# The reciprocal root of three layer normalizations: Newton steps on VectorE in the place of Sqrt on ScalarE and RECIPROCAL on VectorE

## What is computed

```python
def _ln(x, g, b):
    m = jnp.mean(x, axis=-1, keepdims=True)
    v = jnp.mean((x - m) ** 2, axis=-1, keepdims=True)
    return (x - m) * jax.lax.rsqrt(v + EPS) * g + b      # EPS = 1e-05
...
h = _ln(x, pw_g[pathway_ids], pw_b[pathway_ids])
h = _ln(h, cp_g[compartment_ids], cp_b[compartment_ids])
t = _ln(x, tm_g[time_steps], tm_b[time_steps])
s = _ln(x, ms_g[scale_type], ms_b[scale_type])
cat = jnp.concatenate([w[0] * h, w[1] * t, w[2] * m, w[3] * n, w[4] * r, w[5] * s], axis=-1)
return _ln(silu(cat @ int_W1 + int_b1) @ int_W2 + int_b2, int_g, int_be)
...
x = x + attention(cond(x));  x = x + experts(stage(x))
```

## Time and profile before

| | |
|---|---|
| median of 3 runs | 2525.4 us (2524.65 to 2525.51) |
| the profiled execution | 2525.69 us |
| its span | 2523.9 us |
| mean granted PE clock | 0.853 |
| PE busy | 2141.4 us (85%) |
| DVE busy | 1360.4 us (54%) |
| ACT busy | 978.8 us (39%) |
| POOL busy | 858.3 us (34%) |

### The profile page before, as it was taken

The page is one execution under the profiler, slowest core; times in us unless marked ns, Lnnn a source line. Parts: engine busy times, 40 slices in busy tenths (PEclk is TensorE's granted clock), DMA queues, the critical chain, the costliest instruction groups (busy, mean ns, idle before and its releaser), DMA issues. The chain is left out here.

```text
span 2523.9 us, 33767 instructions
## 1 busy us (share of the span) xinstructions
PE 2141.4 (85%) x11902; PEld 1378.9 (55%) x11902; DVE 1360.4 (54%) x3618; ACT 978.8 (39%) x2423; POOL 858.3 (34%) x586
## 2 busy tenths in 40 slices
PE   6518989889889989989988988989999589798987
PEld 5305555555555555555555555556778445454545
DVE  2355766766766766766766665442111055555545
ACT  2004445535535535535535535632222133333231
POOL 0161535534534535435435432041000232424121
PEclk9557698888788788778778778999999789898989
DMA  7100021020020020020020022042445420302000
GB/s 253 44 5 14 1 70 26 1 86 26 1 86 26 1 86 26 1 86 26 1 86 26 1 76 68 1 170 72 149 161 197 150 71 1 85 0 85 0 30 18
DMA packets 67428, 145.88 MB, mean 58 GB/s; under 512 B 16356, under 2 KB 42075, under 8 KB 62947
## 3 DMA queue, kind: packets, MB, share of 16 engines
q1 hardware_dynamic: 51434, 93.79, 11.0%
q0 software_dynamic: 15872, 50.35, 6.6%
HBM read 114.64 MB, written 29.46 MB: 57 GB/s over the span
## 5 line engine op out<-in xcount | busy, mean ns | idle before, releaser
L1211 ACT ACTIVATE att_buf<-att_buf,nmin 128x384 f32<-128x384 f32 (+3 forms) x512 | 287.6, 562 | 497.1 <-DVE nmin L1571 496.7
L1021 PE MATMUL bank<-kk,qT 32*128 32x512 f32 (+2 forms) x1024 | 330.7, 684 | 42.4 <-DVE nmin L1571 41.7
L772 POOL TENSOR_TENSOR big<-ex_at,kx 128x2048 f32<-128x2048 f32 x64 | 236.2, 3713 | 237.9 <-DVE xt_na L1324 175.3
L1048 PE MATMUL bank<-ident,att_buf 128*128 128x128 f32 x1280 | 245.3, 331 | 20.9 <-ACT att_buf L1219 19.7
L1062 PE MATMUL bank<-att_buf,vp 128*32 128x128 f32 x2560 | 226.9, 316 | 0.0
L719 POOL TENSOR_TENSOR big<-kx 128x1280 f32<-128x1280 f32 x64 | 162.8, 2572 | 177.9 <-ACT kx L1125 156.7
L1560 DVE TENSOR_TENSOR att_buf<-bank,wdiag 128x128 f32<-128x128 f32 x384 | 93.0, 284 | 232.3 <-PE bank L1026 231.1
L1219 ACT COPY att_buf<-bank 128x384 f32<-128x384 f32 (+3 forms) x512 | 209.1, 409 | 14.1 <-PE bank L1062 12.0
L1048 PEld LDWEIGHTS bank<-ident,att_buf 128*128 128x128 f32 x1280 | 182.0, 174 | 34.0 <-ACT att_buf L1211 27.9
L1021 PEld LDWEIGHTS bank<-kk,qT 32*128 32x128 f32 x1024 | 111.2, 224 | 113.0 <-DVE nmin L1571 60.8
L1062 PEld LDWEIGHTS bank<-att_buf,vp 128*32 128x32 f32 x2560 | 139.3, 124 | 60.8 <-issue 50.2
(11 more groups left out here) (349 smaller groups left out, 4144.9 us busy)
## 6 DMA issues: line engine op xcount, KB each, us to landing
big<-in_eW SPq DMA_DIRECT2D x16, 1024.0 KB, 7.9
kk<-in_eW SPq DMA_DIRECT2D x16, 1024.0 KB, 7.5
buf_d<-zero SPq DMA_DIRECT2D x8, 640.0 KB, 7.6
xt_na<-in_xT SPq DMA_DIRECT2D x8, 512.0 KB, 3.4
nA<-in_xN SPq DMA_DIRECT2D x8, 512.0 KB, 3.5
x_d<-x SPq DMA_DIRECT2D x8, 512.0 KB, 3.4
x<-x_d SPq DMA_DIRECT2D x8, 512.0 KB, 4.0
out<-qf SPq DMA_DIRECT2D x8, 512.0 KB, 2.9
```

The source lines that it names most:

```text
L772: pool.tensor_tensor(pv[:, c * P:(c + 1) * P, :].rearrange("p (h d) o -> p o h d", d=DH), spread(ex[:, t, :, 8 * c:8 * c + 8], 3, DH), spr ...
L1021: pe.matmul(bank[u % 2][:, 0:n], qT[r:r + 32, g, i * P:(i + 1) * P], kk[r:r + 32, g, T * i * P:T * i * P + n], start=True, stop=False)
L1048: mm = pe.transpose(bank[3 + u % 2][:, j * P:(j + 1) * P], pr[:, u % NPR, j * P:(j + 1) * P], ident[:])
L1211: act.activation(pr[:, u % NPR, 0:n], pr[:, u % NPR, 0:n], ACT.Exp, scale=-1.0, bias=nmin[:, u % 4:u % 4 + 1], accum_out=rsum[:, i, h:h + ...
```

## The change

ACT no longer takes the root in the three normalizations; the Sqrt activations and the semaphores `varn` and `sdn` are gone. DVE makes the reciprocal root itself, in `moments`, right behind the statistics: it adds eps to the variance, takes a first guess by arithmetic on the number's bits (-0.5 times the bits read as an integer, plus a constant), and betters it by three Newton steps, y <- y (1.5 - 0.5 w y y), of three instructions each. That makes eleven instructions on 128x4 numbers, with a wait for DVE's own last result ahead of each. The reciprocal in `normed` is gone. The slots in `AT` of all other steps are as before.

```diff
--- before.py
+++ after.py
@@ -1142,22 +1142,13 @@
                                                        bias=obcol[:, o:o + 1], scale=pc1[:, 4 + o:5 + o])
 
                                 def router_stream():
-                                    sd = lambda n: act.activation(mv[:, :, 2:3], mv[:, :, 1:2], ACT.Sqrt, bias=eps_ln[:, 0:1])\
-                                        .then_inc(s(f"sd{n}"), 1)
-
                                     def out_of_bank(n):
                                         for m in range(K2):
                                             act.wait_ge(s("cat_mm"), 2 * n + m + 1)
                                             act.copy(cat[:, 2 * n + m, :], bank[SIDE[m]][:]).then_inc(s("cat_ok"), 1)
 
-                                    yield AT["x"]
-                                    act.wait_ge(s("var1"), 1)
-                                    sd(1)
                                     yield AT["kxmm"]
                                     out_of_bank(0)
-                                    yield AT["sd2"]
-                                    act.wait_ge(s("var2"), 1)
-                                    sd(2)
                                     yield AT["t_out"]
                                     out_of_bank(1)
                                     yield AT["h_out"]
@@ -1168,9 +1159,6 @@
                                         yield AT["silu"]
                                         act.wait_ge(s("u_mm"), o + 1)
                                         act.activation(aT3[:, o, :], bank[SIDE[o]][:], ACT.Silu, bias=pc3[:, 6 + o:7 + o]).then_inc(s("u_ok"), 1)
-                                    yield AT["sd3"]
-                                    act.wait_ge(s("var3"), 1)
-                                    sd(3)
                                     yield AT["f_out"]
                                     for m in range(K2):
                                         act.wait_ge(s("fT_mm"), m + 1)
@@ -1330,19 +1318,28 @@
                                     dve.tensor_tensor(nv, nv, spread(rs[:].rearrange("p t h -> p (t h)"), 2, DH), ALU.mult)\
                                         .then_inc(s("on_ok"), 1)
 
-                                def moments(src, var):
+                                def moments(src):
 
                                     for t in range(T):
                                         done(dve.bn_stats(stat[:, t, :], src[:, t, :]))
                                     settle()
                                     for t in range(T):
-                                        last = dve.bn_aggr(mv[:, t, 0:2], stat[:, t, :])
-                                    last.then_inc(s(var), 1)
-
-                                def normed(dst, src, sd, ready=None):
-
-                                    dve.wait_ge(s(sd), 1)
-                                    done(dve.reciprocal(mv[:, :, 3:4], mv[:, :, 2:3]))
+                                        done(dve.bn_aggr(mv[:, t, 0:2], stat[:, t, :]))
+                                    settle()
+                                    w, y, yy = mv[:, :, 2:3], mv[:, :, 3:4], stat[:, :, 0:1]
+                                    done(dve.tensor_scalar(w, mv[:, :, 1:2], LN_EPS, None, ALU.add))
+                                    settle()
+                                    done(dve.tensor_scalar(y.bitcast(I32), w.bitcast(I32), -0.5, 1597463007.0, ALU.mult, ALU.add))
+                                    for _ in range(3):
+                                        settle()
+                                        done(dve.tensor_tensor(yy, y, y, ALU.mult))
+                                        settle()
+                                        done(dve.scalar_tensor_tensor(yy, yy, -0.5, w, ALU.mult, ALU.mult))
+                                        settle()
+                                        done(dve.scalar_tensor_tensor(y, yy, 1.5, y, ALU.add, ALU.mult))
+
+                                def normed(dst, src, ready=None):
+
                                     settle()
                                     for t in range(T):
                                         ins = dve.tensor_scalar(dst[:, t, :], src[:, t, :], mv[:, t, 0:1], mv[:, t, 3:4],
@@ -1363,18 +1360,18 @@
 
                                 def router_stream():
                                     yield AT["var1"]
-                                    moments(x1, "var1")
+                                    moments(x1)
                                     done(dve.tensor_copy(pc3[:], pcol[:, b3, :]))
                                     yield AT["z"]
-                                    normed(nA, x1, "sd1", "z_ok")
+                                    normed(nA, x1, "z_ok")
                                     yield AT["h1"]
                                     for t in range(T):
                                         dve.wait_ge(s(f"gath{t}"), 16)
                                     yield from affine(nB, nA[:], gac[:, :, 0:D], gac[:, :, D:2 * D], AT["h1b"], "h1_ok")
                                     yield AT["var2"]
-                                    moments(nB, "var2")
+                                    moments(nB)
                                     yield AT["h2"]
-                                    normed(nB, nB, "sd2")
+                                    normed(nB, nB)
                                     yield AT["h2a"]
                                     for t in range(T):
                                         dve.wait_ge(s(f"gath{t}"), 32)
@@ -1386,9 +1383,9 @@
                                                                spread(row("b2"), 1, 2), ALU.add))
                                     settle()
                                     yield AT["var3"]
-                                    moments(nB, "var3")
+                                    moments(nB)
                                     yield AT["f1"]
-                                    normed(nB, nB, "sd3", "f_ok")
+                                    normed(nB, nB, "f_ok")
 
                                     q = lambda k: pe8[:, k]
                                     step = lambda ins: (done(ins), settle())
```

## The result

The changed kernel took 2568.56 us (median of 4 runs, 2567.91 to 2570.49), the kernel before 2525.45 beside it (median of 4, 2524.65 to 2536.43). Why the first ratio lies above the quotient of its own medians, the listed times do not show. Over all 25 executions of the kernel before and all 8 of the changed one, the medians are 2525.5 and 2568.6. So the change costs some 43 us. The direction and the place were as forecast; the size, 36.6 us in the forecast of 2562, was too small. By the first ratio, which stands for 2579.7, the time is above the range (up to 2573), by the second and by the medians it is inside. What is wrong in the working can be said term by term.

What follows compares the result with a forecast made beforehand. Only what PE or the end of a pass waits for was taken to count. Terms 21.0 + 0 + 0.8 + 14.7 + 2 = 38.5 on 2525.4 gave 2563.9, set at 2562 us for idle time; range 2535 to 2573.

Steps and rivals of the forecast that it cites:

- the 0.8 of the first normalization: First normalization: DVE's added time hidden in idle time from the third router pass on, +0.8 us from the first two.
- the forecast 3.5 us: Third normalization, each of six full passes: DVE's delay plus L1021 at low clock, 3.5 us (2.4 to 3.9).
- The step of the Newton chain: Dependent DVE steps on 128x4 numbers start 0.21 us apart (0.20 to 0.24 allowed), eleven taking 2.3 us.
- the hold by POOL: Third normalization, full passes: POOL's L772 holds y*y, L1324 +3.0 us; +3.4 if scalar steps are held, +2.4 without hold.
- The second normalization: ACT's removed loads and root against DVE's delay at the next scores: between -1.0 and +0.6 us, taken as 0.
- +2 (0 to 4): Eighth pass: PE's wait for L1452 behind the first normalization grows 1.7 us, other two norms among idle time; +2 taken.
- The seventh pass's 12.9 us: Third normalization, seventh pass: PE's wait of 2.8 us drops the clock, the stretch takes 35.0 us instead of 22.1.
- (a): Rival: the clock does not drop in the seventh pass; 2549 us, chance 0.14.
- (b): Rival: the second normalization gains, PE's wait for the exponentials gone and the clock kept; 2543 us, chance 0.08.
- (c): Rival: faster, since ACT's table loads cost at L1048 in the second normalization, 4.4 us per pass; 2514 us, chance 0.06.
- (d): Rival: no change, the clock rises at its old moment behind the third normalization; 2525 to 2530 us, chance 0.06.
- (e): Rival: dearer, a further clock drop in the seventh pass's second normalization, 13 us more; 2577 us, chance 0.05.

Runs made afterwards that it cites:

- third_only: Changed kernel with Newton steps in the third normalization alone, Sqrt on ACT kept in the first and second; 2562.25 us.
- late_third: Changed kernel with the third normalization's Newton steps moved to the old reciprocal's place in `normed`, and Sqrt throughout the eighth pass; 2523.35 us.
- first_two: Changed kernel with Newton steps in the first and second normalization, Sqrt kept in the third; 2539.27 us.
- eighth_two: Kernel before, with Newton steps only in the first and second normalization of the eighth pass; 2534.37 us.
- seventh_only: Kernel before, with Newton steps only in the third normalization of the seventh pass; 2543.51 us.
- one_step: Changed kernel with one Newton step in place of three, 5 instructions in place of 11 per normalization; 2570.32 us.
- behind_sum: Changed kernel with the third normalization's Newton steps behind the token stream's sum, still ahead of the attention units; 2566.57 us.

## Why the prediction was right or wrong

**The path was right.** The third normalization in the full passes and in the seventh carries most of it: 24.5 and 13.5 of 43.0 us, with 21.8 and 14.7 forecast (the 0.8 of the first normalization included). third_only shows it by itself, late_third shows that it is the place. The sum of 38.5 falls short of the 43.0 by 4.5: 2.7 in the full passes, 3.9 in the eighth pass with the experts, less 1.2 in the seventh and 0.9 in parts that the change does not touch. The 1.9 us that the forecast took off for idle time were not there.

**A full pass came out at the forecast 3.5 us by another way.** The prediction had PE busy at half speed in all of the stretch, so that nothing could be made up. But the clock rises at its old moment and PE makes up 1.5 us of its work; what keeps the pass long is DVE, for which PE waits again (3.90 us instead of 1.93).

**The step of the Newton chain**, 0.21 forecast, is 0.20; the hold by POOL was put at y*y and hits the first step, since a TENSOR_SCALAR on SBUF data is held too. The bound that went with it, +3.4, was the better value: L1312 came 3.23 later, PE waited 4.77 and not 4.5. The Trainium skill (SBUF — State Buffer, "Who interferes with whom") names `tensor_scalar` among the instructions that can enter the mode which locks the shared port; the row of L1330 agrees, 1.18 us beside POOL and 0.17 without. L1405, from which the prediction took its value, is of the other kind that this page names.

**The second normalization** came out at zero in the full passes by the two effects of the sum, in their order: ACT's loads gone, DVE's delay in their place. **The first** is hidden from the third pass on, as forecast, only where a pass begins at half speed: there PE's wait at L991 is 2.7 us before and after, and in the changed kernel's third pass, which begins at full speed, it is 4.20.

**The first full pass was mis-sized:** +6.6 us, where 3.7 were in the sum. In the kernel before, its half-speed stretch behind the third normalization was 17.0 us long, with PE at full speed for 10 us after it; now it is 34.1. Two time windows of the kernel before, then one of the changed kernel:

```profile
470.60:487.60 17.00, 17.00 (x78) 10.31 (x76) 10.30 (x27) 7.58 (x22) 7.35 (x2) 0.50 0.00 1
487.60:497.90 10.30, 8.10 (x70) 5.72 (x66) 7.81 (x21) 4.87 (x16) 6.58 (x2) 1.00 0.00 0
```

```profile
469.20:503.30 34.10, 31.27 (x140) 19.91 (x140) 21.74 (x57) 13.67 (x40) 14.33 (x4) 0.50 0.00 1
```

The prediction took its prices from the fifth pass and had noted only that the first is 3 us shorter, not why. How much the term is worth rests in part on chance: with Sqrt and the same wait of 1.52 or 1.53 us, the first full pass took 182.1, 182.0 and 191.9 us in first_two, eighth_two and seventh_only, with none, none and 30.7 us at half speed behind that wait.

**The step that failed most is the eighth pass's "+2 (0 to 4)".** It counted the delay of DVE's first normalization (1.7 forecast; 1.49 more waiting for PE) and took the other two to stand among idle time. The second does not: DVE's `kk` comes 3.4 us later behind it, and PE waits 2.67 us more at L918. Of the stage, 43 us run at half speed, and 37 before. The stage is 5.9 us longer in the changed kernel and 6.8 on the mean of the runs; eighth_two has 9.9 from this alone. The price of a wait in PE's clock was asked for in the seventh pass, but not in the eighth, where the clock was 0.95 over the stage.

**The seventh pass's 12.9 us were of the right size by a wrong picture.** The prediction took the full passes' stretch of 35 us at half speed over; the trace has two of 13.7 and 13.6 us, and one of 27.3 when the kernel was run again. And "the seventh pass had 0.96 and kept it" is no rule: first_two, with the same 0.96, lost the clock there for 10 us, and over the table the seventh pass takes 163.5 to 173.5 us (mean 168.5) with waits of 0.96, and 173.1 to 181.0 (mean 178.8) with 1.44 and 2.65. The longer wait costs 10 us on the mean.

**The range was too narrow at the top** for a reason that no term shows: it was built on 2525.4 +- 0.4. The kernel before spreads over 29 us in thirteen runs, and one of the four runs of the changed kernel in the second timing was 13 us below the next. The range had left 11 us above the forecast.

**The rivals.** (a) fell with the seventh pass at 0.83, and with seventh_only. (b) and (c) fell with the place at L1021 in the second normalization, where PE's wait changed its name. (d)'s mechanism is what the trace of the fifth pass shows, the clock rising at its old moment though PE started later; what failed of it is that the pass gets shorter, since DVE is late. Against it stood only that PE is busy: it was judged too lightly. one_step and behind_sum show that the clock can give or take several us a pass. (e) came in small: the stretch in the seventh pass's second normalization is 13.7 us instead of 10.2, and 10.2 when the kernel was run again. Its 2577 is counted from 2563.9; from 2562, as (a) and (b) are, it would be 2575.

**Still open** is what sets the length of a stretch at half speed. The same wait of 0.96 us at the same place is followed by none, 10 or 17 us of it in the seventh pass; 1.52 us in the first full pass by none, 17 or 31; waits of 3.57 and 3.67 us by 14 to 31 us in the full passes. The runs show that it depends on more than the wait.

## What to carry to other kernels

A chain moved to another engine is paid for at the place where it stands: put it behind the work that the busiest engine is waiting for, and the same eleven instructions cost 7 us in the full passes instead of 24 (in the faster order of the sums 14 instead of 41, and what is left there comes with the other two normalizations). Where the granted clock falls behind a short wait of PE, that wait is priced with its stretch at half speed, for each pass that has it, those with a full clock first. And look for what already stands in such a wait: an edit of one entry of `AT` that moved 1.2 us of sums out of it gave 35 us by the medians, most of what the change had cost.

## What the runs showed of the hardware that I had not expected

A TENSOR_SCALAR of 128x4 numbers was held for the rest of POOL's long product (1.18 us for 0.17), while a TENSOR_REDUCE of 128x1024 ran beside it in 1.19 us. An ACT table load took 1.283 us, and the removal of 30 of them and 24 activations made ACT's busy time 43 us shorter and the kernel no faster. With 0.56 us less in PE's wait at one place (1.52 to 0.96), the half-speed stretch behind it was 10.2 us long in the fifth pass and not 34.1.
